# A rotated second loop with a new order, and row factors moved into the exponent

## The chip, the cores and the metric

The kernel runs on one core of a Trainium2 chip. The core has five engines that run their own instruction streams and meet only at semaphores: TensorE (PE: matmuls, with the weight loads shown apart as PEld), VectorE (DVE), ScalarE (ACT), GpSimd (POOL) and SyncE (SP), which here only issues DMA transfers. The metric is device time in microseconds, median over runs. On-chip data lies in SBUF (here one large tile, "arena") and in eight PSUM banks of 128 partitions by 512 float32 values ("bank"), into which TensorE writes.

## The reference

Eight sequences of 512 tokens with 128 features go through two layers. The first is latent attention and a mixture of 32 experts. The second, which the change concerns, is a gated delta rule with a short convolution, a mixture of 8 experts, and a residual; beside it a second mixture of 8 experts with a hidden width of 512 is computed on the normalized input and added. Cut to what matters:

```
mixed = silu(causal_dwconv(x @ W_qkv, conv_w))          # 16 blocks of 128 channels, 4 taps
beta  = sigmoid(b);  g = -exp(A_log) * softplus(a + dt_bias)
q, k normalized per head
step: S = S * exp(g);  kv = k @ S;  S = S + k * (v - kv) * beta;  o = q @ S
core = rmsnorm(o) * silu(z);  h = x + core @ W_out
y = h + mixture_8(rms(h));   out = y + mixture_8x512(x)   # gelu experts, top 2 of 8
```

The recurrence is not run token by token. The 512 tokens are four chunks of 128, and within a chunk the step is a triangular system. Its matrix needs, for two tokens i and j, the factor exp(G_i - G_j), the product k_i k_j, and a row factor beta / |k|^2.

## The kernel before

Two loops of eight passes each run one after the other: the first computes layer one for all eight sequences, the second layer two. One pass of the second loop handles one sequence. A Python list, schedule_l1 (lines 133 to 176), names the steps of a pass in order, and each engine emits, step by step, the instructions that it has for that name. So one list sets the order on all engines at once, and each engine works strictly in that order. The steps that the change and the prediction name:

- **qkv m**: TensorE, two matmuls of 128x512 (L692), which ScalarE copies with the fourth tap's factor (L1014). **taps m**: VectorE adds the other three taps for two blocks, six instructions (L1519). **silu m**: ScalarE's Silu (L1021), and for q and k also squares (L1026), which **ssq** sums on TensorE (L716).
- **gg, gc**: VectorE computes g from ScalarE's softplus (L1498, L1499), TensorE makes its cumulated sums (L700 to L702), VectorE copies them out (gT, L1504), and SyncE sends them out to DRAM and back as rows Gam, one row per token on all partitions. **scan**: VectorE subtracts and clips in Gam (L1531), eight instructions. **stat**: row statistics (L1536 to L1543). **gam**: ScalarE's exponentials, of the cumulated sums (eG, L1030) and of Gam (L1033), and GpSimd's multiplication of Gam by the row factor nlam = -beta/|k|^2 (L1165). **prep c**: TensorE's products k k and k q of chunk c (L729), VectorE's multiplication with Gam into NTr and QKD (L1562).
- **sub 0 to 3**: VectorE inverts all 32x32 diagonal blocks at once by substitution (L1575, L1577), on a tile M that SyncE gathers through DRAM; the result goes out through DRAM too and comes back as XT. **inv c**: TensorE, ScalarE, VectorE and GpSimd (L1175) put the blocks together to inverses of 128x128. **sw, so1, kt, sdl, ss, so2, nrm, ct, swo**: the recurrence over chunks.
- **cz c**: TensorE (L737) and ScalarE's Silu (L1040) of z; **cv c**: transposed v (L459, L1053). **wfT**: transposed weights of the experts.
- **fh f, gelu f, fo f** (helper ffn): the 32 hidden blocks of the wide mixture: TensorE (L871), ScalarE's Gelu (L1100), TensorE (L881). **facc e**: VectorE adds expert e with its weight (L1684). The experts' weights come by DMA into a ring of two (wring, L405).
- **h1 to h5, moe1, down1**: residual, normalization, router and the small mixture of this layer. **gn, gx, gT, gz, gr, gzT, gba, gend**: normalization, routers and decay inputs of the next pass, already made at the end of this one. `ahead_of_loop` (L331) makes those of the first pass.

Semaphores count up over the passes; `at(b, n, k)` is the count after n events of pass b + k. On every engine the second loop begins at step 0 of the list and jumps back after the last. In the first loop VectorE's part is already rotated (L1420 to L1424): the loop's jump stands in the middle of a pass, the first half of pass 0 stands ahead of the loop and the second half of the last pass behind it.

## Time and profile before

| | |
|---|---|
| Median of 3 runs | 3134.11 us (3131.25 to 3145.35) |
| Profiled execution, its own time | 3141.66 us |
| Its span | 3139.9 us |
| Mean granted TensorE clock | 0.887 of full speed |
| TensorE busy | 2691.1 us, 86% |
| VectorE busy | 2042.6 us, 65% |
| ScalarE busy | 1185.7 us, 38% |
| GpSimd busy | 382.3 us, 12% |

All durations come from the one profiled execution. The second loop takes the stretch from about 1180 us to the end. A row of the timeline has a start, a duration, the engine, the line of the kernel, the operation, what it writes and reads, the count of merged instructions, and in brackets how long the engine was idle before it and what ended that. "issue" there means that nothing the profile shows was waited for. "x8" on matmuls counts records, and a float32 matmul leaves two. Idle time of an engine costs only where the others wait for it.

### The profile page before, as it was taken

What the parts mean: (1) busy time and instruction counts of PE and PEld (TensorE: products, weight loads), DVE (VectorE), ACT (ScalarE), POOL (GpSimd) and SP (SyncE); (2) the same over time, 40 slices, a digit from 0 to 9 for tenths busy, and PEclk for the clock granted to TensorE, in tenths of its full rate; (3) what the DMA queues carried; (4) which work ended last, traced back from release to release, by engine and by line L of the source; (5) the groups of instructions that cost most, each with busy time, mean ns of one, the idle gap of its engine ahead of it and who ended that gap; (6) DMA issues with size and microseconds to landing.
All of it is one profiled execution on the core that took longest, in us unless ns stands there. A gap on an engine that the chain in (4) does not pass through costs nothing.

```text
span 3139.9 us, 48523 instructions
## 1 busy us (share of the span) xinstructions
PE 2691.1 (86%) x15020; PEld 1805.5 (58%) x15020; DVE 2042.6 (65%) x6346; ACT 1185.7 (38%) x2170; POOL 382.3 (12%) x284
## 2 busy tenths in 40 slices
PE   2888888888888867997997897898898898898898
PEld 1434343343433425784785685585596595586587
DVE  4757666585766748558558557657656756845845
ACT  0132231313223125445445444444444444544543
POOL 0000000000000002122112122021120220221211
PEclk8888878897898967998998998997998898899799
DMA  5020101102011121101101101101201201100110
GB/s 139 10 38 7 33 14 25 35 5 37 12 28 21 18 51 41 48 11 58 48 11 58 48 11 49 57 8 48 61 1 55 54 8 55 43 19 28 54 34 15
DMA packets 133697, 109.63 MB, mean 35 GB/s; under 512 B 76968, under 2 KB 117488, under 8 KB 132944
## 3 DMA queue, kind: packets, MB, share of 16 engines
q1 hardware_dynamic: 130192, 100.01, 12.7%
q10 hardware_dynamic: 3264, 6.82, 0.6%
q8 instruction: 100, 1.64, 0.2%
q14 instruction: 141, 1.16, 0.1%
HBM read 86.62 MB, written 20.19 MB: 34 GB/s over the span
## 4 chain that ended last, share of the span: by engine, by line
PE 62%; issue 18%; DVE 11%; DMA 3%; ACT 3%; SPq 2%; POOL 1%; DVEq 0%; ACTq 0%; POOLq 0%
PE bank L871 7%; PE bank L881 7%; PE bank L459 5%; DMA arena<-scrk 3%; DVE arena L1519 3%; PE bank L716 2%; PE bank L610 2%; PE bank L737 2%; PE bank L819 2%; PE bank L555 2%; PE bank L782 2%; PE bank L777 2%; PE bank L765 2%; PE bank L540 2%; PE bank L769 2%
## 5 line engine op out<-in xcount | busy, mean ns | idle before, releaser
L881 PEld LDWEIGHTS bank<-wring,arena 128*128 128x128 f32 x2048 | 269.1, 192 | 109.5 <-issue 107.2
L871 PE MATMUL bank<-arena,wring 128*128 128x512 f32 x512 | 294.8, 666 | 25.9 <-ACT arena L1100 25.9
L1100 ACT ACTIVATE arena<-bank,w_b 128x512 f32<-128x512 f32 x256 | 175.1, 687 | 274.2 <-PE bank L871 273.9
L1519 DVE SCALAR_TENSOR_TENSOR arena<-bank,w_convw,arena 128x511 f32<-128x511 f32 (+2 forms) x384 | 254.8, 740 | 34.6 <-ACT arena L1014 34.5
L881 PE MATMUL bank<-wring,arena 128*128 128x128 f32 x2048 | 271.1, 276 | 0.0
L973 ACT ACTIVATE arena<-bank 128x512 f32<-128x512 f32 x136 | 81.4, 599 | 494.7 <-PE bank L540 441.9
L459 PE MATMUL bank<-w_ident,arena 128*128 128x128 f32 (+2 forms) x1164 | 178.5, 293 | 86.4 <-DVE arena L1266 35.7
L1372 DVE CUSTOM_DVE_ANT_0 bank<-bank,arena 128x128 f32<-128x128 f32 (+3 forms) x512 | 249.2, 492 | 0.0
L982 ACT ACTIVATE arena<-bank 128x512 f32<-128x512 f32 (+1 forms) x384 | 171.1, 535 | 148.9 <-PE bank L597 147.1
L459 PEld LDWEIGHTS bank<-w_ident,arena 128*128 128x128 f32 (+2 forms) x1164 | 135.9, 141 | 118.6 <-issue 66.6
L692 PE MATMUL bank<-arena,w_Wqkvz 128*128 128x512 f32 x256 | 152.7, 733 | 45.0 <-DVE arena L1519 26.1
L1066 ACT ACTIVATE arena<-bank 128x512 f32<-128x512 f32 (+1 forms) x256 | 118.7, 488 | 136.2 <-PE bank L777 69.3
L570 PE MATMUL bank<-arena 48*128 48x128 bf16 (+3 forms) x512 | 110.7, 317 | 64.7 <-DVE arena L1372 36.0
L555 PE MATMUL bank<-arena 128*128 128x128 f32 x1088 | 161.7, 293 | 2.7 <-DVE arena L1357 2.7
L1684 DVE SCALAR_TENSOR_TENSOR arena<-bank,arena 128x128 f32<-128x128 f32 x224 | 63.1, 344 | 154.5 <-PE bank L881 152.7
L540 PE MATMUL bank<-arena 128*128 128x512 f32 x272 | 156.3, 659 | 8.1 <-ACT arena L973 8.1
L326 DVE TENSOR_TENSOR tick<-nhalf 128x1 f32<-128x1 f32 x600 | 94.1, 157 | 93.0 <-PE bank L570 86.4
L543 PE MATMUL bank<-arena 128*128 128x512 f32 x272 | 152.2, 644 | 0.0
L570 PEld LDWEIGHTS bank<-arena 48*128 48x128 bf16 x512 | 34.1, 93 | 200.5 <-DVE arena L1372 92.3
L555 PEld LDWEIGHTS bank<-arena 128*128 128x128 f32 x1088 | 135.6, 196 | 22.8 <-issue 11.3
L1175 POOL TENSOR_TENSOR arena<-arena,w_blk 128x512 f32<-128x512 f32 x64 | 79.8, 1268 | 509.5 <-PE bank L765 358.8
L1165 POOL TENSOR_TENSOR arena<-arena 128x512 f32<-128x512 f32 x64 | 92.3, 1475 | 352.2 <-ACT arena L1033 224.6
(273 smaller groups left out, 5209.3 us busy)
## 6 DMA issues: line engine op xcount, KB each, us to landing
wring<-in_w_last SPq DMA_DIRECT2D x64, 512.0 KB, 3.3
arena<-scrg SPq DMA_DIRECT2D x32, 512.0 KB, 5.4
arena<-scrq SPq DMA_DIRECT2D x108, 64.0 KB
arena<-scrk SPq DMA_DIRECT2D x108, 64.0 KB
scrn<-arena SPq DMA_DIRECT2D x64, 64.0 KB, 1.9
arena<-scrn SPq DMA_DIRECT2D x8, 512.0 KB, 3.6
scrx<-arena SPq DMA_DIRECT2D x8, 512.0 KB, 2.6
arena<-scrx SPq DMA_DIRECT2D x64, 64.0 KB, 2.1
```

The costliest lines, as they stand in the source:

```text
L459: return nc.tensor.transpose(dst, src, W["ident"][0:k, 0:k])
L540: mm(bk[:, :], W["gate0"][:, p, :] if p < PR0 else W["sg"][:], xnT, start=True, stop=True).then_inc(*s["p_gate"].up)
L543: mm(bk[:, :], W["up0"][:, p, :] if p < PR0 else W["su"][:], xnT, start=True, stop=True).then_inc(*s["p_up"].up)
L555: last = mm(bank[7][:, t * P:(t + 1) * P], HID[:, p % 2, t * P:(t + 1) * P], W["down0"][:, p, :] if p < PR0 else W["sd"][:], start=(p == 0 ...
L570: mm(bk[:, 0:w], QS[o:o + KROWS, h // 2, qt * P:(qt + 1) * P], KS[o:o + KROWS, h // 2, 0:w], start=True, stop=True, tile_position=(o, 0)). ...
L692: mm(bk[:, :], W["Wqkvz"][:, m * P:(m + 1) * P], zT, start=True, stop=True).then_inc(*s["p_qkv"].up)
L871: mm(bank[HBANK[f]][:, :], wring[:, e % 2, k * P:(k + 1) * P], xn1T, start=True, stop=True).then_inc(*s["p_fh"].up)
L881: last = mm(bank[OBANK[e]][:, t * P:(t + 1) * P], GH[:, f % 2, t * P:(t + 1) * P], wring[:, e % 2, FC * P + k * D:FC * P + (k + 1) * D], s ...
L982: fn(PT[:, slot, col:col + w], bank[SBANK[n % 4]][:, 0:w], ACT.Exp, scale=float(HD) ** -0.5).then_inc(*s["a_p"].up)
L1100: fn(GH[:, f % 2, :], bank[HBANK[f]][:, :], ACT.Gelu_apprx_tanh, bias=W["b1"][:, f:f + 1]).then_inc(*s["a_gh"].up)
L1372: v.tensor_tensor_reduce(bk[:, 0:w], bk[:, 0:w], W["maskq"][:, S - w:S], 1.0, PAD, ALU.add, ALU.max, mx[:, col:col + 1]).then_inc(*s["v_ma ...
L1519: ins = v.scalar_tensor_tensor(out=cv[:, k:S], in0=bank[2 + m % 4][:, 0:S - k], scalar=W["convw"][:, m, 3 - k:4 - k], in1=cv[:, k:S], op0= ...
```

## The change

Four things are changed, all in the second loop.

1. schedule_l1 has a new order for the part ahead of the inverses and for the end of a pass, with other PSUM banks for some expert steps.
2. On TensorE, ScalarE and VectorE the loop is rotated as VectorE's part of the first loop is: TensorE's jump stands ahead of cz 0, ScalarE's ahead of gelu 6, VectorE's behind sub 3. SyncE fetches the first two experts of the next pass at the end of this one.
3. gend is split into gfe (exponential and row sums of the router), gab (decay inputs) and gpick (choice of two experts); part of its arithmetic moves into gg.
4. GpSimd's multiplications of Gam are gone. ScalarE takes the logarithm of the row factor (now positive, lam, held above 1e-37) and adds it as bias in the exponentials, which become one per head, 128x128 each. The sign is carried on in the constant blk, in the substitution's last operation and in three other places.

```
-HBANK = (7, 4, 5) + (7,) * 17 + (2,) * 12
-OBANK = (6, 3, 6, 3, 6, 3, 5, 3)
+HBANK = (1,) + (7,) * 19 + (2,) * 12
+OBANK = (6, 6, 2, 3, 6, 3, 5, 3)
...
+    order += [("fh", 2), ("gam",), ("prep", 0), ("gelu", 2), ("fo", 2), ("fh", 3), ("prep", 1), ("gelu", 3), ("fo", 3), ("fh", 4)]
+    order += [("prep", 2), ("gelu", 4), ("fh", 5), ("prep", 3), ("gelu", 5), ("rr",), ("facc", 0), ("fo", 4), ("fo", 5), ("taps", 8)]
...
+            def first_experts(b, k):
+                for e in range(2):
+                    if k:
+                        sp_.wait_ge(*s["p_fo"].at(b, FC * (EF - 1 + e)))
+                    sp_.dma_start(wring[:, e, :], w_last[e]).then_inc(*s[f"d_w{e}"].up16)
...
 def gam():
-    act.wait_ge(*s["v_gT"].at(b, 1))
+    act.wait_ge(*s["v_st"].at(b, 1, late))
+    fn(lnlam, lam, ACT.Ln).then_inc(*s["a_lnlam"].up)
+    act.wait_ge(*s["v_gT"].at(b, 1, late))
     fn(eG.rearrange("p a b c -> p (a b c)"), bank[0][:, 0:96], ACT.Exp).then_inc(*s["a_eG"].up)
+    act.wait_ge(*s["a_lnlam"].at(b, 1, late))
     for i in range(2 * NT):
-        act.wait_ge(*s["v_scan"].at(b, i + 1))
-        fn(Gam[:, i, :], Gam[:, i, :], ACT.Exp).then_inc(*s["a_gam"].up)
+        act.wait_ge(*s["v_scan"].at(b, i + 1, late))
+        for j in range(4):
+            h = 4 * (i % 2) + j
+            last = fn(Gam[:, i, j * P:(j + 1) * P], Gam[:, i, j * P:(j + 1) * P], ACT.Exp,
+                      bias=lnlam[:, i // 2, h:h + 1])
+        last.then_inc(*s["a_gam"].up)
...
-def gam():                                  # GpSimd
-    pool.wait_ge(*s["v_st"].at(b, 1))
-    for i in range(2 * NT):
-        pool.wait_ge(*s["a_gam"].at(b, i + 1))
-        g4 = Gam[:, i, :].rearrange("p (a b) -> p a b", a=4)
-        scale = nlam[:, i // 2, 4 * (i % 2):4 * (i % 2) + 4].unsqueeze(2).broadcast_to((P, 4, P))
-        tt(g4, g4, scale, ALU.mult).then_inc(*s["g_gam"].up)
...
+    link(v.tensor_tensor(b4(lam), rk2b, b4(beta), ALU.mult))
+    v.tensor_scalar(lam, lam, 1e-37, None, ALU.max).then_inc(*s["v_st"].up)
...
+            turn = L1.index(("cz", 0))                      # TensorE; ScalarE: ("gelu", 6)
+            ahead_of_loop(gT, gr, gzT, gba, first_part)     # VectorE: behind ("sub", 3)
+            with pe.Fori(0, LOOPS - 1) as b:
+                second_part(b, 0)
+                first_part(b, 1)
+            out_of_loop(second_part, LOOPS - 1)
```

What stood on TensorE in the decay part (L729 is prep, L881 is fo, L692 is qkv), from prep 1's second half on:

```order
L729 MATMUL bank<-arena 128x256 x2
L876 ISA
L881 MATMUL bank<-wring,arena 128x128 x4
L692 MATMUL bank<-arena,w_Wqkvz 128x512 x2
L676 REGISTER_ALU
L729 MATMUL bank<-arena 128x256 x2
L676 REGISTER_ALU
L729 MATMUL bank<-arena 128x256 x2
```

What stands there now, from the last qkv on (L738 is prep, L888 is fo, L878 is fh, L700 is qkv):

```order
L700 MATMUL bank<-arena,w_Wqkvz 128x512
L878 MATMUL bank<-arena,wring 128x512
L738 MATMUL bank<-arena 128x256 x2
L688 REGISTER_ALU
L738 MATMUL bank<-arena 128x256 x2
L883 REGISTER_ALU
L888 MATMUL bank<-wring,arena 128x128 x4
L878 MATMUL bank<-arena,wring 128x512
L688 REGISTER_ALU
L738 MATMUL bank<-arena 128x256 x2
L688 REGISTER_ALU
L738 MATMUL bank<-arena 128x256 x2
```

fo 2 (the first L888) and fh 3 moved in between prep 0 and prep 1; before, fo 0 stood behind prep 1.

ScalarE's end of the decay part before (L1033 the exponentials of 128x512, L1100 gelu):

```order
L1030 ACT_TABLE_LOAD
L1030 ACTIVATE arena<-bank 128x96
L1032 REGISTER_ALU
L1033 ACTIVATE arena<-arena 128x512
L1032 REGISTER_ALU
L1033 ACTIVATE arena<-arena 128x512
```

And now (L1052 the logarithm, L1054 eG, L1060 the exponentials per head, L1129 gelu; of eight groups of four the first and the last are shown):

```order
L1052 ACT_TABLE_LOAD
L1052 ACTIVATE arena<-arena 128x32
L1053 REGISTER_ALU
L1054 ACT_TABLE_LOAD
L1054 ACTIVATE arena<-bank 128x96
L1055 REGISTER_ALU
L1057 REGISTER_ALU
L1060 ACTIVATE arena<-arena 128x128 x4
...
L1060 ACTIVATE arena<-arena 128x128 x4
L1124 REGISTER_ALU
L1129 ACT_TABLE_LOAD
L1129 ACTIVATE arena<-bank,w_b 128x512
```

The logarithm with a table of its own stands ahead of eG, and 8 exponentials became 32.

TensorE around its jump, now (L700 is qkv 14, L888 fo 7, L746 cz):

```order
L700 MATMUL bank<-arena,w_Wqkvz 128x512
L883 REGISTER_ALU
L888 MATMUL bank<-wring,arena 128x128 x4
L957 REGISTER_ALU
L957 COMPARE_AND_BRANCH
L746 MATMUL bank<-w_Wqkvz,arena 128x512 x2
L878 MATMUL bank<-arena,wring 128x512
```

Before, the jump stood between the last matmul of a pass and qkv 0 of the next.

## Rows read from the trace of the kernel before

**Rows 1.** The page, busy time: engine, microseconds, share, instructions.
```profile
PE 2691.1 (86%) x15020; PEld 1805.5 (58%) x15020; DVE 2042.6 (65%) x6346; ACT 1185.7 (38%) x2170; POOL 382.3 (12%) x284
```

**Rows 2.** Timeline of VectorE, L1487, once at the end of each pass.
```profile
1185.70 0.12 DVE L1487 TENSOR_SCALAR arena<-arena 128x32 f32<-128x32 f32 x1
...
1425.17 0.12 DVE L1487 TENSOR_SCALAR arena<-arena 128x32 f32<-128x32 f32 x1
...
1912.00 0.12 DVE L1487 TENSOR_SCALAR arena<-arena 128x32 f32<-128x32 f32 x1
...
2154.12 0.12 DVE L1487 TENSOR_SCALAR arena<-arena 128x32 f32<-128x32 f32 x1
...
3137.04 0.12 DVE L1487 TENSOR_SCALAR arena<-arena 128x32 f32<-128x32 f32 x1
```

**Rows 3.** Windows of one pass: length, busy time by engine, granted clock, DMA share, GB/s.
```profile
1912.00:1924.00 12.00, 5.13 (x15) 2.87 (x16) 6.63 (x30) 7.41 (x11) 0.00 (x0) 0.89 0.34 113
1936.00:1945.00 9.00, 7.70 (x23) 5.50 (x24) 8.56 (x11) 6.31 (x11) 2.78 (x2) 0.50 0.00 0
2022.00:2103.00 81.00, 80.52 (x652) 76.37 (x652) 44.00 (x126) 33.32 (x82) 19.70 (x17) 1.00 0.02 8
```

**Rows 4.** Timeline behind a jump back: second loop, and first loop.
```profile
1912.85 3.69 PE L692 MATMUL bank<-arena,w_Wqkvz 128*128 128x512 f32 x8 [2.51 <-issue]
1918.16 4.03 DVE L1519 SCALAR_TENSOR_TENSOR arena<-bank,w_convw,arena 128x511 f32<-128x511 f32 x6 [3.61 <-ACT arena L1014]
...
1008.41 0.69 DVE L1389 COPY arena<-bank 128x512 f32<-128x512 f32 x1 [2.31 <-issue]
```

**Rows 5.** Timeline of the set-up: TensorE, VectorE and GpSimd.
```profile
1922.57 0.64 PE L700 MATMUL bank<-arena,w_upto 128*128 128x32 f32 x2 [6.02 <-DVE arena L1499]
...
1936.32 4.55 DVE L1531 TENSOR_TENSOR_SCAN arena<-arena,w_floor 128x512 f32<-128x512 f32 x4
...
1941.97 6.96 DVE L1531 TENSOR_TENSOR_SCAN arena<-arena,w_floor 128x512 f32<-128x512 f32 x4
1942.22 11.54 POOL L1165 TENSOR_TENSOR arena<-arena 128x512 f32<-128x512 f32 x8 [43.29 <-DVE arena L1543]
...
1956.00 5.10 DVE L1562 TENSOR_TENSOR arena<-bank,arena 128x512 f32<-128x512 f32 x8 [2.18 <-PE bank L729]
```

**Rows 6.** Groups of instructions, L1074 on ScalarE: busy us, mean ns of one.
```profile
L1074 ACT ACTIVATE arena<-bank,arena 128x128 f32<-128x128 f32 x24 | 6.5, 383 | 2.0 <-PE bank L800 2.0
```

**Rows 7.** Timeline, ScalarE: L1074's eight in a row, and a table load before gelu.
```profile
2049.74 2.18 ACT L1074 ACTIVATE arena<-bank,arena 128x128 f32<-128x128 f32 x8 [0.68 <-PE bank L800]
...
1949.61 1.28 ACT L1100 ACT_TABLE_LOAD   x1
...
1950.91 1.27 ACT L1100 ACTIVATE arena<-bank,w_b 128x512 f32<-128x512 f32 x2
```

**Rows 8.** Timeline of TensorE: cz behind idle time and without it; sums of squares.
```profile
1977.48 6.27 PE L737 MATMUL bank<-w_Wqkvz,arena 128*128 128x512 f32 x8 [5.07 <-DVE arena L1508]
...
2010.84 3.95 PE L737 MATMUL bank<-w_Wqkvz,arena 128*128 128x512 f32 x8
...
2421.94 10.24 PE L716 MATMUL bank<-w_ones,arena 128*128 128x1 f32 x48
```

**Rows 9.** Timeline from the second taps to the inverses.
```profile
1961.02 15.84 DVE L1519 SCALAR_TENSOR_TENSOR arena<-bank,w_convw,arena 128x511 f32<-128x511 f32 x24
...
1980.18 0.19 DVE L1575 TENSOR_TENSOR arena<-arena 128x31 f32<-128x31 f32 x1
...
1989.81 1.12 PE L871 MATMUL bank<-arena,wring 128*128 128x512 f32 x2
...
1991.71 1.13 PE L871 MATMUL bank<-arena,wring 128*128 128x512 f32 x2
...
2005.70 0.21 DVE L1577 TENSOR_TENSOR arena<-arena 128x31 f32<-128x31 f32 x1
...
2022.27 1.04 PE L459 MATMUL bank<-w_ident,arena 128*128 128x128 f32 x8
```

346 lines of the change are left out of this document (189 added, 157 removed).

## The prediction, made before the changed kernel ran

> **What bounds the kernel now.** I read the page's busy shares first: TensorE 86%, VectorE 65% [rows 1]. A mean over stages, so next the second loop pass by pass. The instruction L1487 runs once a pass, at its end, and its starts give the length of each [rows 2]: 239.5 us for the first (1185.70 to 1425.17), which is entered without a jump back, 242.1 us for the one that begins at 1912.00, and (3137.04 - 1425.17) / 7 = 244.55 us as mean of the other seven. The change touches only this loop: 1,960 of 3,140 us. All times below are those of the pass that begins at 1912.
>
> By windows the pass has two characters [rows 3]. From 2022 to 2103 (inverses and recurrence) TensorE is busy 80.5 of 81 us at clock 1.00; nothing that the change does there is cheaper or dearer, so I leave it out. In the first 12 us it is busy 5.1 us, and from 1936 to 1945 it runs at clock 0.50, the lower of its two levels (1.2 of 2.4 GHz). Up to about 1983 the set-up is a chain VectorE - ScalarE - TensorE; from there to 2022 TensorE works off the last experts at one pair of steps (fh, fo) per 1.90 us [rows 9], while VectorE does the substitution.
>
> The timeline shows what the chain waits for. The jump back costs TensorE 2.5 us (idle, "issue") and VectorE up to 3.6 us (its row names ScalarE; part of it is the jump) [rows 4]; the first pass, without one, is 5 us under the mean [rows 2]. In the first loop, whose VectorE part is already split, the jump leaves 2.3 us. TensorE then waits 6.0 us for g (L700) [rows 5].
>
> **The order at the two places that matter.** At the start of a pass TensorE now issues two expert steps behind the first qkv, and has no jump there (it moved ahead of cz 0, VectorE's behind sub 3, ScalarE's ahead of gelu 6). In the decay part, gelu 2 stands behind all exponentials on ScalarE, and on TensorE fo 2, which needs gelu 2, stands ahead of prep 1, 2 and 3. Before, the expert step between prep 1 and prep 2 had its gelu early.
>
> **Part 1: start of the pass.** The splitting of gend lets gab go ahead of the last accumulate: a_sp at 1912.2 instead of 1913.4. No jump: qkv 0 starts near 1910.7, not 1912.85. ScalarE's two copies end at 1913.5, VectorE has g at 1913.8 and starts taps 0 then, not at 1918.16: 4.3 us. g now goes ahead of taps 0, so TensorE makes the cumulated sums under taps 0, and the second taps start at 18.15 and not 24.5: 6.4 us earlier. From there it is VectorE at 4.05 us per taps step in both (24 in 15.84 [rows 9]); ScalarE's queue (copies, Silu, Square, two gelus and one more table load) still keeps up in my walk, with 0.2 us to spare at taps 6. The scan's first half starts at 1930.3 (was 1936.3).
>
> **Part 2: row factors in the exponent.** Removed: 8 GpSimd multiplications, 11.5 us of GpSimd [rows 5], beside VectorE's second half of the scans. Those four take 6.96 us, the first four, with GpSimd idle, 4.55 us: 2.4 us come back. Scans end at 1940.45 (were done at 1948.9): 8.4 us ahead. Added on VectorE: a maximum of 128x32, 0.2 us. Added on ScalarE: one Ln (0.25) with its table load (1.3), and 32 exponentials of 128x128 for 8 of 128x512. The trace has no such exponential; the nearest are L1074's, 128x128 with a per-partition factor: 0.38 us each alone, eight in 2.18, so 0.27 us each in a row [rows 6, 7]. 32 cost 8.7 us. Bounds: 0.14 (a quarter of a long one's pitch) gives 4.4, 0.38 (no overlap) gives 12.2. ScalarE: last copies 1935.8, Ln done 37.4, Exp table 38.6, eG 38.9, factors 1 to 8 ready from 40.0 to 47.5, gelu table 48.8, gelu 2 at 49.5.
>
> On the table loads the row shows a load at 1949.61 and the gelu behind it at 1950.91: 1.30 us for a switch [rows 7]. The Trainium skill ("ScalarE: Activation LUTs", What ACT_TABLE_LOAD costs) has 1.28 us of load plus a drain of 1.38 us, 2.66 us for every switch, which speaks against this change, since it goes from 12 loads per pass to 16. By that rule the four would cost 5.5 us more of ScalarE per pass, two of them on the chain; by the row no drain is seen between the two instructions, and it is the row that the sum uses.
>
> **Part 3: what the saved time runs into.** prep 0 is over at 1943. TensorE stands from 1941.1 to 49.7 before fo 2 (8.6 us), and VectorE has no prep 1 to do. Behind it: fo 2 and fh 3 at half clock 3.4 us (after its 5 us idle L737 took 6.27 us for what takes 3.95 at full clock [rows 8]); prep 1, fo 3, fh 4, prep 2, fh 5, prep 3 at 0.9, 0.9, 0.9, 1.9, 0.9, 1.9 us, so prep 3 leaves VectorE at 1963.5. Before it was 1961.0 (the second four of prep end at 1956.00 + 5.10 [rows 5]). So the 8.4 us gained are used up, and 2.4 more, inside this one part.
>
> **Part 4: from prep 3 to the inverses.** Before: 61.2 us (1961.0 to 2022.27), bound by TensorE. Now three expert pairs and qkv 8 and 10 lie ahead of prep 3, so TensorE would be through at about 2015.3, and VectorE is the later one: expert sum 0 (1.1), four taps steps 16.0 with 0.8 of waiting, clearing 1.1, substitution 25.7 as before (it starts at 1980.2 and ends at 2005.9 [rows 9]): it ends at 2008.5. cz 2 must wait until the block inverses are written out (2.6 us on the page, scrx<-arena): 2011.2; then cz 3, cv 0, gelu 19 with its table, fo 19, wfT: inverses start at 2019.9, 56.4 us behind prep 3. The jumps of VectorE (2.3 us) and TensorE (2.8 us) end before their next work could begin, so I cost them at nothing; if that cover were gone they would be worth 2 to 3 us a pass. The next experts are fetched behind v_mid, a full tail ahead of use: nothing. Negating blk and turning subtract into add changes operands only: nothing.
>
> **The sum.** Against this pass: +2.4 in parts 1 to 3, -4.8 in part 4: -2.4, so 239.7 us. The passes from 2154 on are longer than this one ((3137.04 - 2154.12) / 4 = 245.7 us [rows 2]), since the clock stayed low through their first 26 us (in one, 48 short matmuls took 10.24 us [rows 8]); with TensorE fed from 1910.7 to 1918.4 I expect that not to happen, so the comparison is with the mean: 244.55 - 239.7 = 4.85 us by 7 passes = 34 us. First pass: 0. The program ends 1 us later (out_ready follows gpick). TensorE idles some 4 us before the inverses; the L737 rows price such a start at 2.3 us, I take a quarter, 0.6 x 8 = 5. Together -34 + 1 + 5 = -28. On the profiled execution's own 3141.66 us that is 3114; it lies 7.5 us over the median, so I forecast 3106.
>
> **Rivals.**
> (A) The stop is shorter than I walk it. If the exponentials run at 0.14 us, gelu 2 comes 4.4 us sooner and prep 3 with it; all of it counts, since TensorE is through only at 2015.3. 9.2 us x 7 + 4.4 - 6 = 63 us: 3071. For it: TensorE has work left to give; against: L1074's rows.
> (B) TensorE's work is the same to the instruction, and the front's gain is only slack. If prep 3 comes 3 to 4 us later than I say, or VectorE's 0.2 us of spare in part 1 does not hold, each pass is as long as now: 3125 to 3142. The table drain would, by my walk, add 1.5 to 2.7 us a pass and ends here too.
> (C) Slower, by one mechanism: TensorE stands 8.6 us at fo 2 and its clock does not come back through prep 1 to 3 (in a slow pass it stayed low for 26 us with TensorE nearly always busy). prep 2, prep 3, fo 3, fh 4, fh 5 at half clock: 6.3 us more, less 2 hidden by VectorE; and the first inverses at half clock, 2.3. 6.6 x 8 = 53 us: 3159. It decides from 3.5 us a pass on. For it: the 48 matmuls; against: prep 0 of the old order ran at full clock after a low stretch.
> That the multiplications' removal does nothing is excluded by the 4.55 and 6.96 rows; that it does everything (8 x 2.4 = 19 us) is within the forecast.
>
> **Chances.** Forecast 0.42 (3090 to 3122), A 0.20, B 0.21, C 0.17. The range of eight in ten is 3045 to 3158: it takes in A and nearly all of C. This kernel's measurement tells 0.5%, 16 us, from no change. Faster than 3118: most of the forecast and all of A, 0.59. Within 16 us: B and the forecast's upper end, 0.24. Slower: C, 0.17.
>
> **What would show it.** Starts of taps 0 less than 4 us behind the last accumulate, and no idle 6 us before the cumulated sums: part 1. Second scans at 1.14 us pitch, not 1.74: part 2. TensorE idle 7 to 10 us before fo 2, waiting for gelu 2: part 3. VectorE idle less than 2 us from prep 3 to the substitution's end, and cz 2's Silu released by the write-out: part 4. A pass of 240 us at a steady clock. I am wrong if gelu 2 is not what TensorE waits for, if the exponentials' pitch is far from 0.27, or if the clock in the inverses falls below 1.00.

## The result and the profile after

The changed kernel took 3186.48 us (median of 4 runs, 3169.55 to 3196.03) against 3139.57 for the kernel before on the same chip: a ratio of 1.0142, 95% interval 1.0102 to 1.0182. It is slower by 1.4%, where I forecast 3106 us with a range up to 3158. Run again, unaltered, beside the kernel before on another occasion, it gave 1.0144 (1.0108 to 1.0180). Chips and occasions move the kernel before between medians of 3126 and 3145 us, so times are compared only as ratios to the kernel before on the same occasion.

The first rows to read are the busy shares of the page and the ends of the passes. This is the changed kernel's page:

```profile
PE 2689.4 (84%) x15020; PEld 1802.4 (56%) x15020; DVE 2025.2 (63%) x6351; ACT 1250.5 (39%) x2402; POOL 290.1 (9%) x220
```

TensorE has the same 15020 instructions as before [rows 1] and the same busy time. ScalarE has 65 us more, GpSimd 92 us less, VectorE 17 us less. Less work in sum, and a longer program: waits, then. The last write of the expert weights (L1536 here) answers to L1490 of before and marks the passes. Timeline of VectorE, L1536:

```profile
1204.96 0.19 DVE L1536 TENSOR_TENSOR arena<-pad,arena 128x32 f32<-128x32 f32 x1
...
1948.02 0.19 DVE L1536 TENSOR_TENSOR arena<-pad,arena 128x32 f32<-128x32 f32 x1
...
2200.13 0.19 DVE L1536 TENSOR_TENSOR arena<-pad,arena 128x32 f32<-128x32 f32 x1
...
2944.73 0.19 DVE L1536 TENSOR_TENSOR arena<-pad,arena 128x32 f32<-128x32 f32 x1
...
3190.52 0.19 DVE L1536 TENSOR_TENSOR arena<-pad,arena 128x32 f32<-128x32 f32 x1
```

Eight passes in 1985.6 us, 248.2 each; the same instruction of the kernel before spans 1951.3, 243.9 each. That is 34.3 of the 54.3 us by which the two profiled spans differ. Another 16.9 us lie ahead of the second loop, in code that is the same; the repeated run had them the other way round (its second loop begins at 1182.8, earlier than the 1188.1 of before), so they are chance. The last 3.1 us lie behind the last pass, where the forecast had 1.

Now the places that the forecast spoke of. Timeline of TensorE, changed kernel, pass from 1948: the stop in the decay part, then cz 2, cz 3 and the inverses:

```profile
1969.73 3.76 PE L700 MATMUL bank<-arena,w_Wqkvz 128*128 128x512 f32 x4
1973.28 1.53 PE L878 MATMUL bank<-arena,wring 128*128 128x512 f32 x2
1977.37 3.48 PE L738 MATMUL bank<-arena 128*128 128x256 f32 x8 [2.56 <-ACT arena L1054]
1988.70 2.08 PE L888 MATMUL bank<-wring,arena 128*128 128x128 f32 x8 [7.85 <-ACT arena L1129]
...
1996.99 1.89 PE L738 MATMUL bank<-arena 128*128 128x256 f32 x8
...
1999.58 2.15 PE L738 MATMUL bank<-arena 128*128 128x256 f32 x8
...
2051.86 1.88 PE L746 MATMUL bank<-w_Wqkvz,arena 128*128 128x512 f32 x4
2056.96 3.78 PE L746 MATMUL bank<-w_Wqkvz,arena 128*128 128x512 f32 x4 [3.22 <-ACT arena L1069]
...
2068.09 2.05 PE L774 MATMUL bank<-arena 128*128 128x128 f32 x16 [0.25 <-ACT arena L1095]
```

fo 2 (the first L888) starts after 7.85 us of waiting for gelu 2 (L1129), as forecast (8.6). The two rows of L738 below it are prep 2 and prep 3, at full clock. What I had not counted comes later: cz 3 stands 3.2 us, runs at half clock (3.78 us for what took 1.88 just before), and the inverses begin only at 2068.09. The same stretches on ScalarE:

```profile
1973.53 0.69 ACT L1036 ACTIVATE arena<-bank,w_convw 128x512 f32<-128x512 f32 x1 [1.02 <-PE bank L700]
1974.23 1.28 ACT L1052 ACT_TABLE_LOAD   x1
1975.52 0.23 ACT L1052 ACTIVATE arena<-arena 128x32 f32<-128x32 f32 x1
1975.77 1.28 ACT L1054 ACT_TABLE_LOAD   x1
1977.06 0.25 ACT L1054 ACTIVATE arena<-bank 128x96 f32<-128x96 f32 x1
1977.21 9.44 ACT L1060 ACTIVATE arena<-arena 128x128 f32<-128x128 f32 x32
1986.66 1.28 ACT L1129 ACT_TABLE_LOAD   x1
1987.96 0.69 ACT L1129 ACTIVATE arena<-bank,w_b 128x512 f32<-128x512 f32 x1
...
2055.01 1.28 ACT L1069 ACT_TABLE_LOAD   x1 [3.16 <-DMA scrx<-arena]
```

Between the last copy (L1036) and gelu 2 ScalarE works without a gap: two table loads, the Ln, eG, 32 exponentials in 9.44 us (0.295 each), a third table load. The whole block waits for that last copy, and the copy waits for qkv 10 on TensorE (the first row of TensorE above), which runs at half clock: 3.76 us for two matmuls. The last row is the Silu of cz 2: it stands 3.2 us for the write-out of the block inverses and only then loads its table.

VectorE, changed kernel, same pass, with the one GpSimd row that lies beside it:

```profile
1949.56 4.02 DVE L1567 SCALAR_TENSOR_TENSOR arena<-bank,w_convw,arena 128x511 f32<-128x511 f32 x6
...
1970.91 4.56 DVE L1579 TENSOR_TENSOR_SCAN arena<-arena,w_floor 128x512 f32<-128x512 f32 x4
...
2003.05 1.12 DVE L1730 TENSOR_SCALAR arena<-bank,arena 128x128 f32<-128x128 f32 x4
...
2014.70 7.96 DVE L1567 SCALAR_TENSOR_TENSOR arena<-bank,w_convw,arena 128x511 f32<-128x511 f32 x12 [2.67 <-ACT arena L1036]
...
2023.41 2.49 POOL L1214 TENSOR_TENSOR arena<-arena,w_blk 128x512 f32<-128x512 f32 x2 [47.74 <-ACT arena L1043]
...
2023.96 0.76 DVE L1623 TENSOR_TENSOR arena<-arena 128x31 f32<-128x31 f32 x1
2024.76 1.19 DVE L1625 TENSOR_TENSOR arena<-arena 128x31 f32<-128x31 f32 x1
...
2051.15 0.21 DVE L1625 TENSOR_TENSOR arena<-arena 128x31 f32<-128x31 f32 x1
```

Taps 0 starts 1.5 us behind the last write of weights (3.8 before); the second scans run at 1.14 us each, not 1.74 [rows 5]. But prep 3 ends at 2003, 53.5 us behind the first taps, where it was 42.9 in the pass shown before [rows 5, 9], and the substitution's first two instructions take 1.95 instead of 0.38 us [rows 9] beside GpSimd's L1214.

Since single passes differ by the clock, the measure used from here on is a mean over the eight passes of the one trace that each kernel has, read from such rows: microseconds from the start of taps 0 to the start of the first gelu behind the exponentials, the end of prep 3, the end of the substitution, and the first squaring of the inverses (L774; L765 before); and the length of a pass.

| kernel | gelu | prep 3 | subst. | inverses | pass | ratio to before (95%) |
|---|---|---|---|---|---|---|
| before | 34.5 | 45.1 | 89.9 | 107.7 | 243.9 | 1 |
| changed | 38.4 | 52.8 | 100.6 | 116.5 | 248.2 | 1.0142 (1.0102-1.0182) |
| changed, again | 38.0 | 52.1 | 99.4 | 115.0 | 246.4 | 1.0144 (1.0108-1.0180) |
| e1 multiplications back | 31.5 | 45.7 | 93.7 | 109.2 | 241.3 | 0.9968 (0.9939-0.9996) |
| e2 wide, no factor | 31.5 | 45.6 | 93.5 | 109.4 | 241.0 | 0.9942 (0.9911-0.9973) |
| e3 preparations first | 38.5 | 40.4 | 92.1 | 106.1 | 237.6 | 0.9889 (0.9837-0.9940) |
| e4 jumps at the start | 40.4 | 54.8 | 102.4 | 117.3 | 250.8 | 1.0181 (1.0128-1.0234) |
| e5 before + exponents | 36.8 | 48.4 | 93.1 | 110.3 | 246.6 | 1.0072 (1.0041-1.0103) |
| e6 TensorE fed | 38.1 | 52.3 | 99.8 | 115.2 | 246.8 | 1.0089 (1.0061-1.0117) |
| e7 = e3 + multiplications | 31.4 | 37.7 | 90.3 | 104.2 | 236.7 | 0.9824 (0.9778-0.9869) |
| e8 = e3, better order | 35.2 | 38.3 | 88.7 | 103.0 | 235.2 | 0.9762 (0.9708-0.9816) |
| e9 = e8 + multiplications | 31.6 | 38.6 | 88.9 | 104.1 | 235.2 | 0.9803 (0.9762-0.9844) |
| e10 cz 2 later | 38.3 | 52.9 | 100.8 | 111.5 | 242.4 | 1.0003 (0.9984-1.0021) |
| e11 qkv 10 later | 35.2 | 49.7 | 97.6 | 113.4 | 245.3 | 1.0047 (1.0028-1.0066) |
| e12 all of it | 31.8 | 41.9 | 89.8 | 99.7 | 230.4 | 0.9697 (0.9664-0.9729) |
| e14 three steps mended | 31.6 | 45.6 | 93.5 | 103.9 | 235.4 | 0.9828 (0.9785-0.9870) |
| e15 = e10, jumps at the start | 40.1 | 54.7 | 102.7 | 112.6 | 247.7 | 1.0130 (1.0087-1.0173) |

The two traces of the changed kernel lie 1.8 us a pass apart, so a difference of less than 2 us between two kernels' passes proves nothing by itself. The ratio is the second witness: 1% of the program is 3.9 us a pass. It has a blur of its own, for it also holds the stretch ahead of the second loop, which no experiment touches and which takes from 1175.6 to 1205.0 us in these traces.

### The profile page after: what moved, and what is told of

It reads as the page before. It is cut to its first block, busy times and chain, and to the rows that moved or that the text cites. A ratio compares the mean times of both kernels' runs of the same rounds, so it can differ in the third digit from the quotient of the medians.

```text
span 3194.2 us, 48270 instructions
## 1 busy us (share of the span) xinstructions
PE 2689.4 (84%) x15020; PEld 1802.4 (56%) x15020; DVE 2025.2 (63%) x6351; ACT 1250.5 (39%) x2402; POOL 290.1 (9%) x220
## 4 chain that ended last, share of the span: by engine, by line
PE 52%; issue 18%; DVE 16%; ACT 6%; DMA 5%; SPq 2%; POOL 1%; DVEq 0%; ACTq 0%; POOLq 0%
PE bank L472 5%; PE bank L888 5%; PE bank L878 4%; DMA arena<-scrk 4%; DVE arena L1625 3%; DVE arena L1567 3%; DVE arena L1623 3%; PE bank L828 2%; ACT arena L1060 2%; PE bank L623 2%; PE bank L568 2%; PE bank L791 2%; PE bank L786 2%; PE bank L774 2%; PE bank L778 2%
## 5 line engine op out<-in xcount | busy, mean ns | idle before, releaser
L888 PEld LDWEIGHTS bank<-wring,arena 128*128 128x128 f32 x2048 | 286.5, 207 | 207.2 <-issue 122.8
L888 PE MATMUL bank<-wring,arena 128*128 128x128 f32 x2048 | 293.1, 292 | 97.4 <-ACT arena L1129 76.8
L878 PE MATMUL bank<-arena,wring 128*128 128x512 f32 x512 | 301.3, 675 | 34.5 <-ACT arena L1129 34.5
L1129 ACT ACTIVATE arena<-bank,w_b 128x512 f32<-128x512 f32 x256 | 175.0, 687 | 396.3 <-PE bank L878 396.0
L1610 DVE TENSOR_TENSOR arena<-bank,arena 128x512 f32<-128x512 f32 x128 | 80.1, 684 | 133.4 <-PE bank L738 132.5
L746 PE MATMUL bank<-w_Wqkvz,arena 128*128 128x512 f32 x128 | 86.7, 814 | 69.3 <-ACT arena L1069 65.7
L1214 POOL TENSOR_TENSOR arena<-arena,w_blk 128x512 f32<-128x512 f32 x64 | 79.8, 1267 | 712.3 <-ACT arena L1043 371.5
L878 PEld LDWEIGHTS bank<-arena,wring 128*128 128x128 f32 x512 | 88.8, 209 | 91.4 <-ACT arena L1129 60.8
```

Source lines behind the costliest of these rows:

```text
L878: mm(bank[HBANK[f]][:, :], wring[:, e % 2, k * P:(k + 1) * P], xn1T, start=True, stop=True).then_inc(*s["p_fh"].up)
L888: last = mm(bank[OBANK[e]][:, t * P:(t + 1) * P], GH[:, f % 2, t * P:(t + 1) * P], wring[:, e % 2, FC * P + k * D:FC * P + (k + 1) * D], s ...
L1129: fn(GH[:, f % 2, :], bank[HBANK[f]][:, :], ACT.Gelu_apprx_tanh, bias=W["b1"][:, f:f + 1]).then_inc(*s["a_gh"].up)
```

## The experiments

**e1, the row factors back on GpSimd.** The theory from the rows above (S): the 32 exponentials stand in front of gelu 2, fo 2 stands behind gelu 2 and ahead of prep 1 to 3 on TensorE, so ScalarE's longer block delays VectorE. Rivals: the new order is late by itself (O), or the clock (K).

```diff
-                        for j in range(4):
-                            last = fn(Gam[:, i, j*P:(j+1)*P], ..., ACT.Exp, bias=lnlam[:, i // 2, h:h + 1])
+                        fn(Gam[:, i, :], Gam[:, i, :], ACT.Exp)          # ScalarE, 8 x 128x512
+                        tt(g4, g4, scale, ALU.mult)                      # GpSimd, 8 x 128x512
```

> The changed kernel with the row factors back on GpSimd (8 Exp of 128x512 without bias, 8 GpSimd multiplications, no Ln); order, loops and signs as in the changed kernel (3186 us). Theory S (the 32 exponentials hold up gelu 2, fo 2 and the preparations behind them, and VectorE's substitution with them): in a pass that starts its taps at 0, gelu 2 comes near 33 instead of 38.5 us, prep 3 ends near 46 instead of 53.5, passes are 6 to 8 us shorter, 3120 to 3140 us, although the scans' second half goes back to 1.74 us each. Rival O (the new order itself is what is late: the last copies, the taps and the substitution behind the preparations): under 2 us a pass, 3170 to 3190. Rival K (the clock drops wherever TensorE has gaps, whatever their cause): also 3170 to 3190, the low stretches move but stay as long.

6.9 us a pass came back, 1.7% of the program by the ratios: S. The end of the substitution moved by the same 6.9 us (100.6 to 93.7), so it came through VectorE, as S says. Timeline of VectorE, ScalarE and GpSimd in this kernel, one pass:

```profile
1935.60 4.56 DVE L1580 TENSOR_TENSOR_SCAN arena<-arena,w_floor 128x512 f32<-128x512 f32 x4
...
1938.79 1.28 ACT L1052 ACT_TABLE_LOAD   x1
...
1940.23 4.25 ACT L1055 ACTIVATE arena<-arena 128x512 f32<-128x512 f32 x8
1944.50 1.28 ACT L1122 ACT_TABLE_LOAD   x1
1945.80 0.69 ACT L1122 ACTIVATE arena<-bank,w_b 128x512 f32<-128x512 f32 x1
...
1940.93 8.02 POOL L1205 TENSOR_TENSOR arena<-arena 128x512 f32<-128x512 f32 x8 [40.02 <-ACT arena L1055]
```

Eight wide exponentials take 4.25 us; between the last copy and gelu 2 there are 7.0 us instead of 13.7. And my expectation that the scans would go back to 1.74 us was wrong: in the new order the multiplications begin when the scans are over. They take 1.00 us each there, not the 1.44 of before [rows 5], and the scans keep their 1.14 (4.56 for four). The gain that I credited to the removal of the multiplications had already come from the order. So the order and the loops alone are worth 2.6 us a pass (241.3 against 243.9, ratio 0.9968), and the exponentials turn that into a loss.

**e2, wide exponentials and no factor at all.** This kernel leaves the row factor out of the computation.

```diff
-                    fn(lnlam, lam, ACT.Ln)
+                        fn(Gam[:, i, :], Gam[:, i, :], ACT.Exp)          # no bias, nothing multiplies it in
```

> The changed kernel with 8 Exp of 128x512 without bias instead of 32 of 128x128 with it, and without the Ln and its table load; the row factor is left out of the computation, nothing multiplies it in. Theory S: ScalarE is busy 5 us instead of 12.5 between the last copies and gelu 2, which comes 7 to 8 us sooner; prep 3 ends 9 to 10 us sooner, a pass is 8 to 9 us shorter, 3110 to 3125 us. Rivals O and K: 3165 to 3190. Against the kernel with multiplications back it tells what the multiplications themselves cost, by theory S 1 to 2 us a pass.

241.0 us a pass against 241.3, and medians of ten runs each of 3130.8 and 3129.5 us: the eight GpSimd multiplications cost nothing that can be measured in this order (1.0 us a pass by the ratios, whose intervals overlap). Removing them bought nothing, and the exponentials that replaced them cost 6.9 us. I had expected 1 to 2 us for the multiplications, and 8 to 9 us a pass in all (3110 to 3125 us), where 7.2 came.

**e3, the preparations ahead of gelu 2 and fo 2.**

```diff
-("gam",), ("prep", 0), ("gelu", 2), ("fo", 2), ("fh", 3), ("prep", 1), ("gelu", 3), ("fo", 3), ("fh", 4), ("prep", 2), ...
+("gam",), ("prep", 0), ("prep", 1), ("prep", 2), ("prep", 3), ("gelu", 2), ("fo", 2), ("fh", 3), ("taps", 8), ("gelu", 3), ...
```

> The changed kernel, exponentials with bias kept, with all four preparations ahead of gelu 2 and fo 2, and taps 8 straight behind them (first expert sum behind taps 8, silu 8 and qkv 12 ahead of gelu 6 and 7). Theory S: the preparations then run at the pace of the exponentials (2.4 us per block of rows) and prep 3 ends about 13 us sooner, near 40 us behind the first taps; VectorE's substitution ends 10 us or more sooner, TensorE becomes the later one, a pass is 5 to 10 us shorter, 3105 to 3150 us. Rival E (the cost is the exponentials' own ScalarE time, wherever they stand): within 2 us a pass, 3170 to 3190. Rival K: TensorE now stands 9 to 10 us in one piece, its clock stays low longer through the experts behind, and the time is 3186 or above.

With the exponentials unchanged, prep 3 ends at 40.4 instead of 52.8 us and a pass takes 237.6, 10.6 less: the forecast of S (a little more, even), and E falls. The cost was not ScalarE's time by itself but what stood behind it. TensorE does stand longer in one piece, and K's loss does not come: by the trace's record of the granted clock, a pass has 29 us at the low level instead of 46 (40 in the repeat of the changed kernel).

**e4, the jumps back at the start of the pass.**

```diff
-            turn = L1.index(("cz", 0))       # TensorE; ScalarE: gelu 6; VectorE: behind sub 3
+            turn = 0
```

> The changed kernel with the jumps back of TensorE, ScalarE and VectorE all at the start of a pass, as before the change (new order and exponentials kept). If the moved jumps are worth what I counted in part 1, TensorE and VectorE start 2.5 to 4 us later in 7 passes: 3205 to 3215 us. Rival: VectorE's wait between the scans and the preparations takes it up, since the exponentials hang on ScalarE's last copies: 3183 to 3192. If the moved jumps themselves are what made the kernel slower (they stand in front of cz 0 and behind the substitution): 3160 to 3175.

250.8 against 248.2 us a pass; the 3202.8 us lie just under the 3205 that I had counted, and the intervals of the two ratios overlap. e15 settles it.

**e5, the exponents alone, in the order and loops of before.**

```diff
+                    fn(lnlam, lam, ACT.Ln)
-                        fn(Gam[:, i, :], Gam[:, i, :], ACT.Exp)
+                            last = fn(Gam[:, i, j*P:(j+1)*P], ..., ACT.Exp, bias=lnlam[:, i // 2, h:h + 1])
-                        tt(g4, g4, scale, ALU.mult)
```

> The kernel before, in its own order and with its own loops, with only the exponent part of the change (Ln, 32 Exp of 128x128 with bias, no GpSimd multiplications, the signs). In the changed kernel these exponentials cost 6.9 us a pass (248.2 against 241.3 us with the multiplications back). If they cost it in any order where expert steps stand behind them (theory S: here gelu 0, fo 0 and, behind fo 0, prep 2 and 3 on TensorE): gelu 0 comes 6 to 7 us later than before (34.5 us behind the first taps), prep 3 ends 4 to 6 us later (45.1 before), passes of 248 to 250 us, 3175 to 3190 us. If they cost only in the new order, where prep 1 to 3 stand behind fo 2 (rival N): here prep 0 and 1 don't wait, passes within 1.5 us of before, 3135 to 3155 us.

2.7 us a pass, 0.7%: between the two, and outside both ranges. In the old order only prep 2 and 3 stand behind fo 0 on TensorE, and the first gelu moved by 2.3 us, not 6 to 7, since the copies of qkv 10 stand behind the exponentials there and the Ln can start with the statistics. Timeline of e5, ScalarE's Ln and VectorE's second scans:

```profile
2219.32 0.23 ACT L1031 ACTIVATE arena<-arena 128x32 f32<-128x32 f32 x1 [2.55 <-DVE arena L1544]
...
2219.20 4.57 DVE L1531 TENSOR_TENSOR_SCAN arena<-arena,w_floor 128x512 f32<-128x512 f32 x4
```

The Ln waits for the statistics (L1544). And here, where the multiplications used to run beside the second scans, their removal does bring those from 6.96 [rows 5] to 4.57 us: what the forecast counted exists in the old order. The new order makes the same exponentials two and a half times as dear (6.9).

**e6, TensorE fed in its stop.** 40 transposes go to a free bank; their results are not used.

```diff
+                    if f == 2:
+                        need("v_prep", 1)
+                        for j in range(40): tr(bank[0][:, ...], xn1[:, j % NT, :])
```

> The changed kernel with 40 transposes of the identity's shape on TensorE in its 7.8 us stop ahead of fo 2 (into a bank that is free there; nothing reads them). They take 4.4 us at clock 1.00, 8.7 us at 0.50 (0.11 us each at 1.00 by the rows of such transposes). If a part of the loss is the low clock behind the stop (theory K as an addition to S), the clock between fo 2 and the experts behind prep 3 stays up, prep 3 ends 1.5 to 2 us sooner (51.9 instead of 53.6 in the passes where it was late), a pass is 2 to 6 us shorter, 3140 to 3170 us. If the clock behind the stop costs nothing that VectorE does not hide: 3180 to 3190; and 3190 to 3200 if the transposes only delay fo 2.

1.4 us a pass (246.8), less than the 2 that I had set as the bound, with a ratio whose interval overlaps that of the changed kernel; the repeat of the changed kernel shows 246.4 without it. As a gain it is inconclusive. But the feeding did what it was meant to: between 26 us behind taps 0 and the end of prep 3 the low level takes 7.7 us a pass instead of 13.0 (12.4 in the repeat), and prep 3 ends only 0.5 us sooner. So the low clock behind the stop is not the loss: my rival C asked 6.6 us of it. This says nothing of the low clock elsewhere.

**e7, e3 with the multiplications back.**

```diff
 (e3's order)
-                            last = fn(Gam[:, i, j*P:(j+1)*P], ..., ACT.Exp, bias=lnlam[:, i // 2, h:h + 1])
+                        fn(Gam[:, i, :], Gam[:, i, :], ACT.Exp)          # ScalarE, 8 x 128x512
+                        tt(g4, g4, scale, ALU.mult)                      # GpSimd, 8 x 128x512
```

> The kernel with the preparations ahead of gelu 2 (3110 us, passes of 237.6) and in it the GpSimd multiplications back instead of the 32 exponentials. Gelu 2 is ready 7 us sooner, but fo 2 stands behind prep 3 on TensorE, and prep 3 needs the eighth multiplication (1.44 us each, from about 28.5 us behind the first taps: 40 us, prep 3 over at 42.5 instead of 40.4). Theory S: with the preparations first the exponentials are no dearer than the multiplications: within 2 us a pass, 3100 to 3125 us. Rival E (ScalarE's 7 us count in any order): 6 us a pass less, 3060 to 3070 us.

236.7 against 237.6 us: with the preparations first, ScalarE's 7 us are worth 0.9, which is within what two traces of one kernel differ by. Prep 3 ended at 37.7, not 42.5, since the multiplications again ran behind the scans, at 1.00 us and not 1.44. The ratio (0.9824 against 0.9889) says more than the passes, 2.6 us a pass; but in the two traces 16.3 of the 23.8 us between them lie ahead of the second loop, and the intervals overlap.

**e8, a better order around it.** In e3, qkv 10 goes behind prep 0 (and its copies behind the exponentials), gelu 6 ahead of silu 8, ScalarE's jump ahead of cz 0, TensorE's ahead of prep 0.

```diff
-("ssq", 6), ("qkv", 10), ("scan", 0), ...   ("gam",), ("prep", 0), ("prep", 1), ...
+("ssq", 6), ("scan", 0), ...   ("gam",), ("prep", 0), ("qkv", 10), ("prep", 1), ...
```

> The kernel with the preparations first, and in it: qkv 10 and ScalarE's copies of it behind prep 0 and behind the exponentials (they held up the Ln by 3 us), gelu 6 ahead of silu 8, the jump back of ScalarE ahead of cz 0 and that of TensorE ahead of prep 0, where it stands anyway. By theory S the exponentials end 3 us sooner, prep 3 at 37.5 us behind the first taps; TensorE's stop of 4.7 us before gelu 6 shrinks to 1 to 2, and the 2.7 us ahead of cz 0 go: 3 to 7 us a pass, 3055 to 3090 us. Rival (TensorE's low clock takes what is gained, as its stop in the exponentials is now longer in front of gelu 2): 3100 to 3115.

2.4 us a pass, 0.9762: a kernel faster than before by 2.4%, with the exponentials kept. Prep 3 ends 2.1 us sooner, somewhat under the 3 expected. The four moves were made together, so what each is worth is not shown. **e9** is the same with the multiplications:

> The last kernel (preparations first, qkv 10 behind prep 0, jumps moved; 3069 us, passes of 235.2) with the GpSimd multiplications back instead of the 32 exponentials. With the preparations first they took 0.9 us a pass off (236.7 against 237.6). Here the exponentials start 3 us sooner, so the multiplications have the scans' pace and the statistics to wait for (from about 23 us behind the first taps, eight of 1.44 us: 35, prep 3 over at 37.5 against 38.3). If the multiplications are the better form in every order: 0.5 to 2 us a pass less, 3050 to 3066 us. If the exponentials pay once nothing waits behind them but the preparations: 3070 to 3085 us.

235.2 in both: no difference. As the exponentials start sooner here, the multiplications ran partly beside the scans again (they last 1.41 us in the median, 1.04 in e7), and prep 3 ended at 38.6, 0.3 later than with the exponentials. Where nothing waits behind them but the preparations, the two forms come out equal. The 3071 us lie at the lower edge of my second case, which had expected the exponentials to be ahead.

**e10, the last expert steps ahead of cz 2.**

```diff
-ffn(1) + [("cz", 2), ("cz", 3), ("cv", 0)] + ffn(1) + ffn_rest()
+ffn(2) + ffn_rest() + [("cz", 2), ("cz", 3), ("cv", 0)]
```

> The changed kernel with the last expert steps (fh 19, gelu 19, fo 18 and 19) ahead of cz 2, so that TensorE and ScalarE have work while the block inverses are written out (3.1 to 3.5 us; ScalarE waited 3.9 us a pass for it in 7 of 8 passes, and its table load of 1.3 us stands behind the wait). If this exposed wait is what made the stretch from the end of the substitution to the inverses 16 us where I forecast 12.7: that stretch is 12 to 14 us, a pass 2 to 4 us shorter, 3155 to 3172 us. If the stretch is bound by the clock alone, or by VectorE's expert sums: 3180 to 3190.

The largest surprise: 5.8 us a pass by the traces (4.0 against the repeat of the changed kernel) and the whole 1.4% by the ratio (1.0003), from one group of steps moved. From the end of the substitution to the inverses it is 10.8 us instead of 16.0. Timeline of e10, TensorE and ScalarE, pass from 2392, where the substitution ends at 2493.7:

```profile
2494.07 2.10 PE L888 MATMUL bank<-wring,arena 128*128 128x128 f32 x16
2496.01 1.88 PE L746 MATMUL bank<-w_Wqkvz,arena 128*128 128x512 f32 x4
2499.31 1.98 PE L746 MATMUL bank<-w_Wqkvz,arena 128*128 128x512 f32 x4 [1.42 <-ACT arena L1069]
2501.13 2.35 PE L472 MATMUL bank<-w_ident,arena 128*128 128x128 f32 x20
2503.93 2.05 PE L774 MATMUL bank<-arena 128*128 128x128 f32 x16 [0.45 <-ACT arena L1095]
...
2497.36 1.28 ACT L1069 ACT_TABLE_LOAD   x1 [2.40 <-DMA scrx<-arena]
```

ScalarE still waits for the write-out, and its table load still stands behind that wait: cz 3 starts 5.6 us behind the end of the substitution, as in the changed kernel's pass from 1948. Two things have gone. The work that used to be queued behind cz 3 (fh 19, fo 18 and fo 19, with gelu 19 and its table load between them) is done while VectorE ends the substitution and while the result is written out. And as TensorE has that work, it reaches cz 2 later and its stop before cz 3 is 0 to 1.4 us in seven of the eight passes, where it was 3.0 to 6.0 in the loop of the changed kernel, and cz 3 runs at full clock (1.98 us, not 3.78). In the eighth, the pass from 2147, TensorE stopped 3.2 us and cz 3 ran at half clock, and the same stretch took 13.1 us instead of 10.1 to 11.1. So the price was not the wait as such, which is as long as it was, but what stood behind it and what TensorE did not do in it.

**e11, qkv 10 and its copies behind prep 0**, in the changed kernel, alone.

```diff
-("ssq", 6), ("qkv", 10), ("scan", 0), ...   ("prep", 0), ("gelu", 2), ...
+("ssq", 6), ("scan", 0), ...   ("prep", 0), ("qkv", 10), ("gelu", 2), ...
```

> The changed kernel with qkv 10 and ScalarE's copies of it behind prep 0 and behind the exponentials; nothing else moved. The Ln then starts about 3 us sooner and the two copies (1.3 us) stand in front of gelu 2: gelu 2 comes 1.5 to 2 us sooner (38.4 us behind the first taps now), prep 3 ends 1.5 to 3 us sooner. If the late copies were part of why my forecast missed: 1.5 to 3 us a pass, 3162 to 3175 us. If TensorE's low clock, or VectorE behind prep 3, takes it up: 3180 to 3190.

2.9 us a pass, and the ratio goes from 1.0142 to 1.0047, with intervals that lie apart: the late copies were part of the miss. Gelu 2 comes 3.2 us sooner, where I had expected 1.5 to 2.

**e12, the moves together** (e9's order and its GpSimd multiplications; fo 2 and fh 3 behind prep 1, fo 3 and fh 4 behind prep 2; the first expert sum ahead of taps 8, silu 8 and qkv 12 ahead of taps 10; cz 2 as in e10).

```diff
+("gam",), ("prep", 0), ("qkv", 10), ("prep", 1), ("gelu", 2), ("fo", 2), ("fh", 3), ("prep", 2), ("gelu", 3), ("fo", 3), ...
+ffn(2) + ffn_rest() + [("cz", 2), ("cz", 3), ("cv", 0)]
```

> The kernel of the first run of this set (better order, GpSimd multiplications) with expert steps spread between the preparations again, since gelu 2 is ready early with the short exponent part (fo 2, fh 3 behind prep 1, fo 3, fh 4 behind prep 2), the first expert sum ahead of taps 8, silu 8 and qkv 12 ahead of taps 10, and the last expert steps ahead of cz 2. If TensorE is what ends last: its stops ahead of fo 2 and before the inverses shrink, 2 to 5 us a pass under the first run, 3025 to 3050 us. If prep 3 comes later by the steps between, and VectorE ends last: within 1 us a pass of it.

3035 us, ratio 0.9697 (0.9664 to 0.9729): 3.0% faster than before, 4.4% faster than the changed kernel. It is the best version found, and it is without the exponentials per head. What TensorE waits for in the second loop, by the view of waits (microseconds in all, times, longest): first the changed kernel, then e12.

```profile
PE bank L888 <- ACT arena L1129: 76.8, 16, 9.3
PE bank L746 <- ACT arena L1069: 65.7, 16, 6.0
```

```profile
PE bank L888 <- ACT arena L1122: 33.8, 20, 3.4
...
PE bank L746 <- ACT arena L1062: 22.4, 14, 3.1
```

In the changed kernel fo's wait for gelu (L888) and cz's wait for the Silu (L746) make 142 us of the second loop, 18 a pass; in e12 they are 56. In the kernel before, the largest of this view was this:

```profile
PE bank L737 <- DVE arena L1508: 47.6, 8, 6.7
```

**e13, the changed kernel again**, and **e14, the three steps mended** in it (multiplications, qkv 10 behind prep 0, cz 2 later):

> The changed kernel, unaltered, beside the kernel before. In its first profile 16.9 of the 54.3 us lay ahead of the second loop, in code that the change does not touch, and 34.3 us in the second loop's eight passes (248.2 against 243.9 us each). If the first loop's part is chance (its passes take 133 or 140 us in both kernels): the first loop comes out level or the other way, the passes again at 247.5 to 249, and the ratio at 1.009 to 1.014. If it belongs to the change: again 10 to 20 us ahead of the second loop and a ratio of 1.014 to 1.018.

> The changed kernel with the three steps undone or mended that each took something off alone: GpSimd multiplications instead of the 32 exponentials (6.9 us a pass), the last expert steps ahead of cz 2 (5.8), qkv 10 and its copies behind prep 0 (2.9; with the short exponent part no Ln waits for them, so 0 to 1 here). If these are separate causes: 248.2 - 6.9 - 5.8 - 0.5 = 235 us a pass, 3055 to 3080 us, ratio 0.977 to 0.985. If the first two pay out of one slack (TensorE's last experts before the inverses): 238 to 241 us a pass, ratio 0.988 to 0.998.

e13 gave 246.4 us a pass, nearly 2 us under the first profile and 1.1 under my range; that is how far single traces of one kernel lie apart, and the ratio repeated itself (1.0144). The 17 us ahead of the second loop did not come again, though I had expected a ratio of at most 1.014 for that case. e14 gave 235.4 where the sum of the separate effects was 235, and 0.9828 in the range that went with it: separate causes that add up, not one slack paid twice.

**e15, e10 with the jumps at the start.**

```diff
 (e10's order)
-            turn = L1.index(("cz", 0))       # TensorE; ScalarE: gelu 6; VectorE: behind sub 3
+            turn = 0
```

> The kernel with the last expert steps ahead of cz 2 (passes of 242.4 us, ratio 1.000), with the jumps back of TensorE, ScalarE and VectorE at the start of a pass. The same jumps back cost 2.6 us a pass in the changed kernel's profile (250.8 against 248.2). If that is what moving them is worth: 244.5 to 246 us a pass, ratio 1.006 to 1.012. If it was the clock's doing: within 1 us a pass, ratio 0.997 to 1.003.

5.3 us a pass, ratio 1.0130 against 1.0003, with intervals far apart: more than the 2.6 of e4, and above the upper range that I had given (246 us a pass, 1.012). So the moved jumps are a gain, worth some 5 us a pass in this order. The first taps of e15 start 1.9 us later behind the pass's start. The other 3.4 us come between taps 0 and the inverses (1.1) and behind them (2.3), and go with the clock, 52 us of a pass at the low level against 41; that the clock is their cause was not isolated.

## Why the prediction was wrong

In short: the mechanism of the forecast was right up to prep 3, and its sizes were not. Between taps 0 and the inverses it put a pass 9.1 us too short, 3.1 us up to prep 3 and 6.0 us in part 4, and that turned a forecast gain of 4.85 us a pass into a loss of 4.3.

**Part 1** (start of the pass) held. Taps 0 came 1.8 us earlier behind the last weights in the mean, the tail 2.8 us shorter: 4.6 us, forecast 4.3. The first half of the scans was over when I said. Its last step failed, though: ScalarE's copies of qkv 10 ended 24.7 us behind the first taps, not 22.0, because TensorE ran the last sums of squares and qkv 10 at half clock (3.76 us for two matmuls, about 1.8 more than at full clock). "With TensorE fed from 1910.7 to 1918.4 I expect that not to happen" held for the first 12 us behind taps 0, which have no low clock now (6.7 us before, in the mean), but not behind them: 7.1 us from there to 26 us, where these steps run, and 13.0 from 26 us to the end of prep 3, where before had 3.9. I had walked from a pass with 34 us at the low level; the changed kernel has 46 (40 in the repeat), the kernel before 42 in the mean. The start of the Ln hangs on those copies. Mis-sized by 2.7 us; e11 took 2.9 off.

**Part 2** (exponents): the pitch was 0.295 us against my 0.27, 0.7 us in all. The scans' 2.4 us came back, but in the new order they come back with the multiplications too (e1), which cost nothing measurable there (e2). Only in the old order is it the removal that brings them (e5). The table loads are 1.30 us from load to use here too: the Trainium skill's rule of another 1.38 us of drain for every switch ("ScalarE: Activation LUTs", What ACT_TABLE_LOAD costs) is not borne out by 1974.23, 1975.52 and 1975.77, three rows without a gap.

**Part 3** (what the saved time runs into) was right as a mechanism: TensorE stops 7.8 us at fo 2 (8.6 forecast), VectorE idles, prep 3 ends late. It was late by 3.1 us more than forecast (52.8 against 49.7), nearly all of it the copies and the pitch. That this arrangement was a choice, and that the same exponentials cost 0.9 us a pass by the traces with the preparations first (e3, e7), the forecast did not ask. Nor did it ever set them against the multiplications in the new order, where they are the whole loss: 6.9 us.

**Part 4** (prep 3 to the inverses) is where the sign turned. I forecast 56.4 us for what took 61.2 before (counted to the row of L459 that lies 1.3 us ahead of the column in the table). By the table it took 116.5 - 52.8 = 63.7, so 62.4 in that count, 6.0 too many. Three terms: VectorE waited 2.3 us in the mean (1.0 to 2.7) for the copies of qkv 12, where I had 0.8; the substitution took 27.4 us, not 25.7, since GpSimd's multiplication (L1214) fell on its first two instructions; and from its end to the inverses the mean was 16.0 us, not 12.7.

For this last I had counted the write-out at 2.6 us (it was 3.4, the median of the changed kernel's page), and behind it cz 3, cv 0, gelu 19 with its table, fo 19 and wfT. What I had at nothing was cz 2's own table load of 1.3 us, which stood behind the wait and not ahead of it; and for the low clock after the stop, at which cz 3 took 1.8 us more, my sum has 0.6. The last pass of the changed kernel, which stands outside the loop, shows it by chance: it has the same steps in the same order, but there the table load went ahead of the wait, TensorE stopped 1.5 us and cz 3 ran at full clock, and it was 12.7 us, my figure. e10 shows something else: the steps that I had counted behind the wait needed not stand there. Moved ahead of it they cost nothing, and the stretch falls to 10.8, under my figure too.

**The sum.** Forecast 239.7 us a pass. Up to prep 3 it is 3.1 us more, from there to the inverses 6.0 more, and from the inverses to the next taps 0 it is 0.8 less than I had (131.6 us): 248.0. Measured 248.2 and, again, 246.4. That e10 and e11 take off nearly the same sum (5.8 and 2.9) is chance, for e10 goes past my figure. The comparison with the mean of before (244.55 over seven passes) took 2.4 us a pass for a steadier clock; the traces have 46 and 40 us a pass at the low level against 42, which does not show it.

**The rivals.** A (exponentials cheaper) had its condition reversed: the pitch was above, not below. B's condition (prep 3 comes 3 to 4 us late and the gain is gone) did occur, 3.1 us, but it did not stop at zero. C had the sign, and about half the size (25 us over the 3134 of before, where 45 came by the ratio), by a mechanism that was not it: prep 2 and 3 ran at full clock in the rows seen, the first inverses too (granted clock 1.00 from 2066 to 2072), and feeding TensorE brought 1.4 us. One of my signs of being wrong did appear: over the inverses and the recurrence together (2066 to 2147) the granted clock was 0.96, not 1.00. The low clock did cost something, but elsewhere, at qkv 10 and at cz 3. My slower side had one mechanism where the loss came from several smaller ones, some in sentences that I had priced at nothing or almost nothing. The range's upper end, 3158, was too low for their sum, and it did not even take in C's own 3159, let alone nearly all of C.

One reading in the forecast was loose: the 48 "short matmuls" of 10.24 us [rows 8] are records, two for each float32 matmul, so 24 matmuls.

Still open: why the passes of one kernel differ (245.8 to 252.1 us in the changed kernel's first trace) with the same instructions. It goes with the low stretches of the clock: of the 5.7 us between the pass from 1948 and the next, 3.8 lie behind the start of the inverses, where the low level takes 10.2 against 3.4 us. What starts these stretches was not isolated. Nor was the table load of cz 2 ever moved alone, so its 1.3 us are read from the rows of the last pass, not from a run.

## What to carry to other kernels

When an engine's block grows, list what stands behind it in every other queue, and ask first whether that order is needed: the same 32 exponentials cost 6.9, 2.7 and 0.9 us a pass in three orders (the last within the scatter of traces). A step placed behind a wait that is sure to end last is paid in full, with its table loads and its clock; put work that is ready ahead of such a wait (5.8 us for one moved group), and price the whole chain behind it, not the wait. And before crediting an edit with a contention that it removes, check whether the other half of the change has already moved the two apart.
